# Row maxima over 97 rows with a zero row, masks in fp32r, one product for several heads, folds in turn, and another order of the streams

## What is computed

```python
scores = jnp.einsum('bqhd,bkd->bhqk', q, k) * scale        # 16 heads, one key head
scores = jnp.where(causal[None, None], scores, min_val)
attn = jax.nn.softmax(scores, axis=-1)
ctx = jnp.einsum('bhqk,bkd->bqhd', attn, v)
...
gate = x @ W_gate + _lora(x, sA_gate, sB_gate, scale) + _expert_lora(...)
up = x @ W_up + _lora(x, sA_up, sB_up, scale) + _expert_lora(...)
hidden = jax.nn.silu(gate) * up
out = hidden @ W_down + _lora(hidden, sA_down, sB_down, scale) + _expert_lora(...)
```

## Time and profile before

| | |
|---|---|
| median of 3 runs | 995.62 us (990.35 to 1001.97) |
| the profiled execution | 999.05 us |
| its span, first to last instruction | 997.3 us |
| mean granted TensorE clock | 0.962 |
| busy: PE / PEld / DVE / ACT / POOL | 938.5 / 672.2 / 614.4 / 315.5 / 310.1 us |
| fill matmuls | 428 |

### The profile page before, as it was taken

One profiled execution on the slowest core, in us unless ns is written; L12 is line 12 of the kernel. 1 busy time (PEld: TensorE's weight loads), 2 busy tenths in 40 slices (PEclk: granted clock), 3 DMA queues, 4 the chain that ended last, 5 costly groups with the idle time before them and its releaser, 6 DMA issues.

```text
span 997.3 us, 13830 instructions
## 1 busy us (share of the span) xinstructions
PE 938.5 (94%) x5362; PEld 672.2 (67%) x5370; DVE 614.4 (62%) x945; ACT 315.5 (32%) x544; POOL 310.1 (31%) x393
## 2 busy tenths in 40 slices
PE   6899998689999899999999899999989999899997
PEld 5665576445567676766687666766668787578885
DVE  2375668778876596766756785765567665332222
ACT  2323532345453116253332234334221521120110
POOL 3634631444770132235400141255114023011110
PEclk9887999698799999999999999999999999999999
DMA  8796625343790933358346533372524455535442
GB/s 288 254 313 236 246 106 131 110 129 131 277 337 18 257 107 114 139 209 300 128 156 152 177 121 123 134 276 99 204 74 185 153 192 206 190 126 193 173 162 90
DMA packets 42917, 174.96 MB, mean 175 GB/s; under 512 B 5404, under 2 KB 8220, under 8 KB 32868
## 3 DMA queue, kind: packets, MB, share of 16 engines
q1 hardware_dynamic: 36804, 119.02, 35.2%
q10 hardware_dynamic: 6048, 55.05, 15.3%
HBM read 127.46 MB, written 33.75 MB: 162 GB/s over the span
## 4 chain that ended last, share of the span: by engine, by line
PE 81%; DVE 6%; issue 3%; ACT 3%; DMA 3%; SPq 2%; POOL 1%; POOLq 0%; DVEq 0%
PE ring L984 12%; PE ring L985 12%; PE ring L986 12%; PE ring L981 5%; PE slots L1056 4%; PE av L1088 4%; PE slots L1074 4%; PE ring L1220 4%; PE den L1088 3%; PE slots L984 3%; PE slots L986 3%; PE slots L985 3%; SPq L608 2%; PE slots L1157 2%; PE slots L1053 2%
## 5 line engine op out<-in xcount | busy, mean ns | idle before, releaser
L776 POOL TENSOR_TENSOR hd_l<-hd,hd_h 128x512 fp32r<-128x512 f32 x44 | 57.3, 1302 | 287.7 <-ACT hd_h L951 287.7
L984 PE MATMUL ring<-xT_h,gu 128*128 128x512 f32 x352 | 143.2, 407 | 0.4 <-DVE gated L1544 0.3
L1338 DVE TENSOR_REDUCE negm<-slots 128x1 f32<-128x384 f32 (+3 forms) x176 | 107.2, 636 | 58.2 <-PE slots L1056 57.2
L985 PE MATMUL ring<-xT_l,gu 128*128 128x512 f32 x352 | 137.6, 391 | 0.0
L986 PE MATMUL ring<-xT_h,gu 128*128 128x512 f32 x352 | 137.5, 391 | 0.0
L853 ACT ACTIVATE probs<-slots 128x512 f32<-128x512 f32 (+1 forms) x176 | 90.7, 556 | 97.4 <-PE slots L1074 97.0
L743 POOL TENSOR_SCALAR_AFFINE_SELECT probs<-probs 128x128 f32<-128x128 f32 (+2 forms) x176 | 67.3, 394 | 125.6 <-ACT probs L853 124.8
L1056 PE MATMUL slots<-kst,qst 96*128 96x128 f32 (+3 forms) x256 | 87.2, 416 | 0.0
L1074 PE MATMUL slots<-qst,kst 98*128 98x128 f32 (+3 forms) x256 | 68.5, 357 | 13.2 <-DMA qst<-negm_hl 12.1
L984 PEld LDWEIGHTS ring<-xT_h,gu 128*128 128x128 f32 x352 | 66.3, 188 | 19.6 <-issue 7.1
L986 PEld LDWEIGHTS ring<-xT_h,gu 128*128 128x128 f32 x352 | 66.1, 188 | 14.6
(11 more groups left out here) (195 smaller groups left out, 1807.8 us busy)
## 6 DMA issues: line engine op xcount, KB each, us to landing
gu<-gu_parts ACTq DMA_DIRECT2D x42, 1280.0 KB, 5.5
dn<-dn_parts SPq DMA_DIRECT2D x12, 1728.0 KB, 7.3
gu_parts<-gu SPq DMA_DIRECT2D x11, 1280.0 KB, 5.5
qst<-qT_h SPq DMA_DIRECT2D x64, 128.0 KB, 2.4
raw_gu<-gu SPq DMA_DIRECT2D x11, 640.0 KB, 7.4
dn_parts<-dn SPq DMA_DIRECT2D x11, 576.0 KB, 7.7
dn<-dn_parts SPq DMA_DIRECT2D x4, 1152.0 KB, 5.2
x_in<-x SPq DMA_DIRECT2D x8, 512.0 KB, 5.7
```

What stands on the lines that cost most here:

```text
L776: pool.tensor_tensor(hd_l[:, i, :], hd[:, i, :], hd_h[:, i, :].bitcast(F32), ALU.subtract).then_inc(hd_lo.sem, 1)
L984: pe.matmul(out_, w_hi_, m_hi_, start=start, stop=False, skip_group_check=True)
L985: pe.matmul(out_, w_hi_, m_lo_, start=False, stop=False, skip_group_check=True)
L1338: dve.tensor_reduce(negm[:, h0:h0 + heads, qt], slot("max", b, g, i)[:, 0, 0:heads * n].rearrange("p (h n) -> p h n", n=n), AX.X, ALU.max, ...
```

## The change

Five edits. (1) A 97th row (`MROW`) goes between the 96 rows and the maxima: zero in `kst`, and in `qst` rows of the identity, which the zeros cancel. The maxima's products run over 97 rows, the scores' over 99. Two more DMAs per `q` step write that row, ahead of the 12. (2) Identity and mask of the maxima are fp32r (`mask_r`) instead of bf16; a bf16 identity (`ident_bf`) stays for fills and transposes. (3) `scores` issues one matmul for all heads of a bank: one of 4 x 128 columns instead of four (16 banks), one of 2 x 256 instead of two (32 banks). (4) `prep_gu` claims both PSUM tiles first and goes from side to side, tile by tile. (5) `TURNS` is another: 439 fills instead of 428, mostly as many short ones, and steps in another order.

```diff
+MROW = KROWS + 1
...
-    "A1A111114111111111114111111414111AA4444111111111111194111141AA1114A14AAAAA1AAA1W41WWAAWAX14XX11X1114X1XXX41XXW"
+    "A11A111411111411111111111AA111111111111111141111111111111111111114111111111111111111111111AA11A11AA11AAA111111"
...
-        mask_bf = sb("mask_bf", [P, 2, P], BF16)
+        ident_bf, mask_r = sb("ident_bf", [P, 1, P], BF16), sb("mask_r", [P, 2, P], F32R)
...
-        q_moved, m_moved = [sig(f"q_moved{i}", 16 * 12) for i in range(2)], [sig(f"m_moved{i}", 32) for i in range(4)]
+        q_moved, m_moved = [sig(f"q_moved{i}", 16 * 14) for i in range(2)], [sig(f"m_moved{i}", 32) for i in range(4)]
...
+                for g in (2 * ep, 2 * ep + 1):
+                    sp.dma_start(qst[KROWS:MROW, 4 * g:4 * g + 4, :].bitcast(F32), mask_r[0:4 * TT, 0, :].bitcast(F32)).then_inc(q_moved[ep].sem, 16)
...
-                for src, row in ((negm_h, KROWS), (negm_l, KROWS + 1)):
+                for src, row in ((negm_h, MROW), (negm_l, MROW + 1)):
...
-                                              (kst[KROWS:P, :].bitcast(F32), 1.0), (ln_eps[:, :], LN_EPS))):
+                                              (kst[KROWS:P, :].bitcast(F32), 1.0), (kst[KROWS:MROW, :].bitcast(F32), 0.0), (ln_eps[:, :], LN_EPS))):
...
-                for side in range(2):
-                    rank_rows = slice(32 * side, 32 * side + RANK)
-                    ps = in_ring.claim(pe, ("prep_gu", f, side), folded_gu, 2 * f + side + 1)
-                    for k in range(KT):
-                        mm = pe.matmul(ps[:, k * P:(k + 1) * P], fold[rank_rows, k * P:(k + 1) * P],
+                ps = [in_ring.claim(pe, ("prep_gu", f, side), folded_gu, 2 * f + side + 1) for side in range(2)]
+                for k in range(KT):
+                    for side in range(2):
+                        rank_rows = slice(32 * side, 32 * side + RANK)
+                        mm = pe.matmul(ps[side][:, k * P:(k + 1) * P], fold[rank_rows, k * P:(k + 1) * P],
...
-                pe.matmul(diagonal, mask_bf[:, 0, :], mask_bf[:, 1:2, :].to_broadcast([P, heads, P]), start=True, stop=False,
+                pe.matmul(diagonal, mask_r[:, 0, :], mask_r[:, 1:2, :].to_broadcast([P, heads, P]), start=True, stop=False,
...
-                    mm = pe.matmul(ps[:, 0, h * n:(h + 1) * n], qst[0:KROWS, 4 * g + h0 + h, qt * P:(qt + 1) * P],
-                                   kst[0:KROWS, 0:n], start=False, stop=True, skip_group_check=True)
+                    mm = pe.matmul(ps[:, 0, h * n:(h + 1) * n], qst[0:MROW, 4 * g + h0 + h, qt * P:(qt + 1) * P],
+                                   kst[0:MROW, 0:n], start=False, stop=True, skip_group_check=True)
...
-                for h in range(heads):
-                    mm = pe.matmul(ps[:, 0, h * n:(h + 1) * n], kst[0:KROWS + 2, kt * P:(kt + 1) * P],
-                                   qst[0:KROWS + 2, 4 * g + h0 + h, kt * P:T], start=True, stop=True, skip_group_check=True)
-                mm.then_inc(t_ps.sem, 1)
+                pe.matmul(ps[:, 0, 0:heads * n].rearrange("p (h n) -> p h n", n=n), kst[0:MROW + 2, kt * P:(kt + 1) * P],
+                          qst[0:MROW + 2, 4 * g + h0:4 * g + h0 + heads, kt * P:T], start=True, stop=True, skip_group_check=True)\
+                    .then_inc(t_ps.sem, 1)
```

More of the change, by code:

```diff
@@ L285 @@
[L285 to L289, removed]
@@ new lines @@
+    "WXWXAX1AXXAXWXXAAAAA11111AA111111AX11XAA1AA1AAAAA41XAAX1AAAAAAAAAAA14111A41111WAAAAAAWA1141AAAA11A4111A11A141A"
+    "11AAAA11AAAWWAAAA4A1AA44AAAAAAAA111AAAAA11AAAWAAAAAAAAAWALWALLA444AL4L4L1L1L41A4AALAA4LLA444LXXLWXLLX4LX4LXXX1"
+    "1LX1XLLXX4LLXALX444X49LAXL1ALLX4LAX1XALLWLXWLWXXALLWLLLLLLXLALWXAXXALAAAAAXALAXAXXLAAAXALLLA4AXLXAAL4ALAAALLAL"
+    "AAAAAAAXALLAAAXXALLLWAAAAXAALLWLLAWXLLWLLLLLAXWXXALAXWLALXX9ALLAALAF9AAAWAAAAALAALAWAALLWWALFFLAAAAFALAAAFAAAA"
+    "FAALALAAWAAAALFAALAAAAAFAFAFAFAAFAFLFALAA1FL111ALAFLFFFFXXXFFXXFFFLFXF1XXFXFFFFLF4XFFFALFFF1XFFFFLAFXFF1XXFFFA"
@@ new lines @@
+    "XXAFFALLFLFXFXAXLFFXXXXFFLLX1LLFAAXFAFLAXFFFFLLALFFLFFFFAFFLLFAFXXLFFLFXFLFFALLXXFALFFFFFAXFFAFFLXLFFXFFXLXLL1"
+    "XLAFXLL1ALFFLLFFFLFFLLFLFAAFFXFAALLALFFAFFLAAFLALAFFFFLALFAAALAFFFALFXFAAAAAXF1ALXFFFAFAFFAXXFLFLFALAAFLFLAAAA"
+    "AFFAAFLLLLAFFLLAFFLLFLALLFLAFFFFFLAFAFFAAFALFFFAFALFAAFAFFALLFFLFLFFALALAAFLAFAFFFLFLAAFFFAAFFLFAAAAAAAAALFFAF"
+    "AFAAFAFAAAFAAAAAFFAAFAFFFLFAFF1LFAFFFFAF1FFFAFFAFFFFAFFXFLFFFXXAFFFXXXFFFXXXFLXFLFFXFAFXFXFXFFXFAFXLFXFLFFFFFX"
+    "XFFFXFFXXAXFAFALLFFFFXFFFFFLLLFFLXAAFXFFFLLFL1LAXLFLFFXFFFXFFXFFLLFLFXAXLXFXFFAFFLLLFFFAFAXLAAAFXFLFXLLFFLLXFF"
@@ new lines @@
+    "FFAAFXLXXLFFLLLLLFLLLAFLFALAFAF1AAFLFFLFFLLFFAAAFLFFL1LAAALAALLAFFLFFFLLAFXFAFFFFFLAAAFFLFLFLFLAFFLLLFFFFLFLFF"
+    "FALFLLFAFALLLLFAFFFAFLFALFLFLFFLFAAAFLLXAXAAFFFFFFFFFALFLAAAALLAAAFFAAFFFAAAAAAFAAFFAFALFAAAAAALFAFAAAAFFAAAAF"
+    "FAFAAAAFAAFFFAAFAAFFAFAFFFFAFAFFFFFFFFFAFAAFFFFFLFAFLLFFFF9FLFFFFFLLFFLFFFFFFFFFFLFLFFFFFFFLFLLFFFFFFFLFFFFLFF"
+    "LFLFFLLFLLLFFFFLFFFLFFFLFLFFFFFLLLFLLFFFFFFFLLFFLFLFFLLLFFFLFLFLFLFFLLFFFFFFFFFLFFLFFFFLLFLLFFFFLFLLLFLFFFFLFL"
+    "FFFFFLFFLFFFLFFFFLFFLLFLLLLLLFFLFLFFLFFFLLFFLFLLFFFFFLFFFFFFFFLFFFFFFFFFFFFLFFFLFFLFFLLFLFLLFFF4FFFFFFFFFFFFFF"
@@ L787, in _ @@
             act.wait_ge(c_loaded.sem, 32)
-            act.activation(mask_bf[:, 0, :], cst[:, :], ACT.Copy).then_inc(masks_ready.sem, 1)
-            act.activation(mask_bf[:, 1, :], masks[:, :], ACT.Copy).then_inc(masks_ready.sem, 1)
+            act.activation(ident_bf[:, 0, :], cst[:, :], ACT.Copy).then_inc(masks_ready.sem, 1)
+            act.activation(mask_r[:, 0, :], cst[:, :], ACT.Copy).then_inc(masks_ready.sem, 1)
+            act.activation(mask_r[:, 1, :], masks[:, :], ACT.Copy).then_inc(masks_ready.sem, 1)
             act.wait_ge(w_loaded.sem, 16)
@@ L974, in _ @@
             pe.wait_ge(c_loaded.sem, 32)
-            pe.wait_ge(masks_ready.sem, 2)
+            pe.wait_ge(masks_ready.sem, 3)
             def fill(n):
@@ L980, in fill @@
                 for _ in range(n):
-                    pe.matmul(ps[:, 0:2 * P], mask_bf[:, 0, :], mask_bf[:, :, :], start=True, stop=True, skip_group_check=True)
+                    pe.matmul(ps[:, 0:2 * P], ident_bf[:, 0, :], ident_bf[:, :, :].to_broadcast([P, 2, P]), start=True, stop=True, skip_group_check=True)
             def three(out_, w_hi_, w_lo_, m_hi_, m_lo_, start, stop):
```

22 lines of the change are left out of this document (7 added, 15 removed).

## The result

The changed kernel takes 1002.78 us (median of 20 runs); the kernel before, measured beside it, 1003.48 us (median of 20). The ratio is 1.0059, 95% interval 1.0031 to 1.0086. Forecast were 979 us and a range of 961 to 1000, so the forecast was wrong. The change makes no difference of 1%: by the ratio it is a loss of 0.3 to 0.9%, by the medians nothing.

The account below looks back on a forecast made before the run. TensorE was taken to bound the kernel from 280 us on, a mixture with 74 us at half clock before. Terms -3 - 6 - 2 + 3.7 + 1.2 - 3 - 8 = -17.1 from 995.6 gave 979 us, range 961 to 1000.

Parts of the forecast that it names:

- the longest wait: TensorE's 8.86 us wait for batch 1's maxima shrinks to 1 to 2 us: -3 us, bounds -15 and +10.
- a new wait behind 300 us: Sign against the forecast: a wait there, where nothing covers it, would break the forecast altogether; no size given.
- rival B: Gain before 280 us is absorbed as waits for VectorE, ScalarE or DMAs: -5 us, 990.5 us, chance 0.26.
- The clock: Before 280 us, fewer waits, shorter folds and fills return part of the half-clock time: -8 us, bounds 0 and -25.
- Rival C: Clock holds 2.4 GHz nearly throughout: -25 us instead of -8, 961 us, chance 0.12.
- Folds in turn: Eleven fold steps: both sides' matmuls overlap throughout, 16 take 0.9 us instead of 1.5: -6 us, bounds 0 and -8.
- Scores: Score banks: one product for four heads pays one weight load, 16 banks x about 0.2: -3 us, bounds -4 and -2.
- Masks: 176 banks of the maxima: fp32r mask product is shorter, its wider weight load hidden under the matmul ahead: -2 us.
- rival A: Load of the fp32r identity lies open at each of 176 banks, 25 us in all: 1005 us, chance 0.10.
- The 97th row: Two more DMAs per query move delay the first maxima of batches 0 to 2: +3.7 us, bounds 0 and +5.
- Fills: 11 more at 0.11 us: +1.2 us; 36 more up to batch 0's first gate product, 25 fewer behind it.
- The base: Median of the kernel before from which the terms were subtracted: 995.62 us, of three runs.

Follow-up runs that it names:

- the new back of the order: Changed kernel with the old order up to the last output product of batch 1's attention, the new order behind it: 999.34 us, ratio 0.9985.
- the front: Changed kernel with the new order up to the last output product of batch 1's attention, the old order behind it: 1001.12 us, ratio 1.006.
- the halves: Kernel before with only the new order: 1020.67 us, ratio 1.0205; changed kernel with the old order, so only the edits: 991.05 us, ratio 0.9937.

## Why the prediction was wrong, step by step

**The step that failed is "the longest wait"**, and in it the sentence "Other waits move too, and the order can't say how far". I gave the whole new order -3 us and bounds of -15 and +10. The runs give it +20 us in the kernel before and +12 with the edits in, outside these bounds. I had followed one wait out of the order and taken it for the order's worth. Most of what the order costs in the kernel before is not even waiting in itself: 18.1 of 24 us in the ledger are half clock on work and 4 are idle time. With the edits in, the ledger shows 6 of the 12: 4 idle, 2 half clock, 3 work, less 3 of fills.

The new waits of the changed kernel are 3.92 us for `negm_hl` at 257, 2.61 for POOL's probabilities at 481, 1.95 at 117, and 1 us more for `hd_l` at 854. None of them stands in the trace of before, so a reading of that trace could not price them. The last sentence of the prediction said what would break it, a new wait behind 300 us. It did come, and the new back of the order costs some 3 to 5 us at the same clock; the larger part, 8 to 10, lies in the front. Which of the new waits costs what wasn't tested one by one.

**Even the wait that went gave nothing.** It is gone in the changed kernel:

```profile
186.34 0.27 ACT L847 ACTIVATE negm_hl<-slots 16x128 fp32r<-16x128 f32 x1 [9.01 <-PE slots L1069]
188.14 0.28 DVE L1348 TENSOR_TENSOR negm_hl<-slots,negm_hl 16x128 fp32r<-16x128 f32 x1
188.49 1.20 SPq L621 DMA_DIRECT2D qst<-negm_hl  x2
...
190.98 0.50 PE L1079 MATMUL slots<-qst,kst 99*128 99x512 f32 x1
```

5 us behind the turn instead of 9, with 25 fills in between, as worked out. The integer product of batch 0 starts at 207.3 us, as it did before: rival B's mechanism, at this place. (The turn itself came 2 us later than before, at 185.93.)

**The clock** (-8). The sign was right, and the median clock rose by 0.012, which is 11 us by the table above, more than I gave. But it is the work of the edits alone: the order by itself lowers it (0.957 to 0.9505), which the forecast has nowhere. And against the profile from which the sum was made, half clock on work fell by only 2.8 us. Rival C's clock without breaks didn't come.

**Folds in turn** (-6). The 16 matmuls take 1.16 us instead of 1.71 at full clock, 0.55 gained, as worked out. In the changed kernel three of the eleven steps lie at half clock, where they take 2.08, more than the 1.71 of before, when all but a bit of one step ran at full clock:

```profile
38.13 1.16 PE L999 MATMUL ring<-fold 8*128 8x128 f32 x16
```

```profile
171.54 2.08 PE L999 MATMUL ring<-fold 8*128 8x128 f32 x16
```

Alone, with one step at half clock, the folds shorten the eleven steps from 18.9 us to 13.7; in the changed kernel they are at 15.7. The ledger gives the folds alone 4.4 us less work and 3.2 less half clock, and 3.3 more idle time; the runs at the same clock are 1 us faster. So the step itself was sized nearly right, and what failed is that it would reach the end of the kernel: much of it came back as waits, as rival B has it.

**Scores** (-3): right, 2.8 in their own matmuls (46.9 to 44.1 at full clock), 4 at the same clock; four heads now take 0.23 us. **Masks** (-2): behind a product of 512 columns the bank of 384 columns takes 0.29 us where it took 0.30:

```profile
414.73 0.22 PE L1059 MATMUL slots<-mask_r 128*128 128x128 f32 x1
414.79 0.39 PE L1062 MATMUL slots<-kst,qst 97*128 97x384 f32 x1
415.01 0.63 PE L1225 MATMUL ring<-y_u,gu 128*128 128x512 f32 x2
```

0.28 from this bank to the next matmul where the earlier trace rows have 0.29. Right behind wide products, and invisible in the whole. The load of the identity did double,

```profile
L1059 PEld LDWEIGHTS slots<-mask_r 128*128 128x128 f32 x176 | 36.0, 204 | 35.3 <-issue 20.6 <-DVE negm L1343 5.5 <-ACT probs L858 2.2
```

204 ns where 104 were, and it lies under the products only where a long one stands ahead. The kernels with and without the mask edit, both with scores and folds in the old order, have the same matmul ahead of each bank. Here it is a short one, `av` with 128 columns, first with the bf16 mask, then in fp32r:

```profile
202.56 0.42 PE L1088 MATMUL av<-probs,v 128*32 128x128 f32 x8
202.91 0.23 PE L1054 MATMUL slots<-mask_bf 128*128 128x128 bf16 x1
202.95 0.48 PE L1057 MATMUL slots<-kst,qst 96*128 96x512 f32 x1
203.36 0.43 PE L1088 MATMUL den<-probs,ones 128*32 128x128 f32 x8
```

```profile
201.19 0.42 PE L1089 MATMUL av<-probs,v 128*32 128x128 f32 x8
201.54 0.33 PE L1055 MATMUL slots<-mask_r 128*128 128x128 f32 x1
201.71 0.45 PE L1058 MATMUL slots<-kst,qst 96*128 96x512 f32 x1
202.09 0.42 PE L1089 MATMUL den<-probs,ones 128*32 128x128 f32 x8
```

From `av` to `den` 0.80 us became 0.90. Of the 176 banks 110 ran at full clock and without a wait in both traces. From the start of the matmul ahead to the start of the one behind, the 28 behind another bank's products are 0.026 us shorter in the mean, those behind products of the feed-forward 0.009 to 0.015, the 11 behind `av`, `den` and the folds 0.09 to 0.10 longer, and the 5 behind the transposes 0.06 longer. In the mean of all 110 that is +0.001 us: the two cancel. So rival A's mechanism is real at one bank in seven, its price of 25 us is excluded, and the term was 0 instead of -2.

**The 97th row** (+3.7): the issues were sized right, 1.2 us in each batch, but in four batches and not in three: with all edits and the old order batch 3 waits 1.49 us instead of 0.32, and in the changed kernel 1.83, where I took it for covered. 4.8 us of idle time, 3.9 by medians. Two more entries stand at the head of the move:

```profile
33.44 1.21 SPq L608 DMA_DIRECT2D qst<-mask_r  x2
34.70 0.68 SPq L612 DMA_DIRECT2D qst<-qT_h  x1
```

**Fills** (+1.2): the count was right, and 10.42 us of them are left behind 280 us, 2.9 less than in the earlier trace rows, as worked out. Idle time there grew by more (28.1 to 33.9 us).

**The base.** 995.62 us was 6 us below what 81 runs give. With the right base the same terms would have given 985, still 18 us below what was measured.

## What to carry to other kernels

A changed order of a full schedule is the largest term and the least known: price it by what it could cost at every place where TensorE is the bound, not by the one wait that it removes, and leave both signs open. Before a wait is called removed, follow every engine of its chain, not only the one that the trace names; here a second one stood behind it. Before a weight load is called hidden, look at the shortest matmul that can stand ahead of it, not at the usual one. Compare runs at the same granted clock as well as medians: a gain by clock and a loss by order cancelled here within 1 us, and only the halves showed both. But don't take a higher mean clock for a gain: where fills raised it by 0.012, the time fell by 2 us.

## What the runs showed of the hardware

A wait of 2.4 to 4.1 us in an otherwise full stage can be followed by TensorE at 1.2 GHz on full work. In the changed kernel, around 325 us:

```profile
320.00:325.00 5.00, 4.84 (x22) 3.68 (x20) 3.94 (x8) 1.74 (x3) 0.00 (x0) 1.00 0.83 182
325.00:329.00 4.00, 0.07 (x1) 0.10 (x1) 0.61 (x2) 0.00 (x0) 0.00 (x0) 0.98 0.86 191
329.00:333.00 4.00, 4.00 (x15) 3.62 (x16) 2.02 (x3) 0.00 (x0) 0.00 (x0) 0.50 1.01 313
333.00:337.00 4.00, 4.00 (x15) 3.39 (x14) 2.92 (x4) 0.63 (x1) 1.30 (x1) 0.66 1.11 243
```

The clock is full in the wait and falls behind it, at 328.9 us. A wait of 2.38 us at 854 in this kernel was followed by 3.4 us at half clock, one of 2.61 us at 481 by none. The wait for the queries of batch 2 was 2.71 us in the kernel with scores and folds and was followed by nothing of the kind (nor were the 2.68 us of the kernel before); in the kernel with the folds alone it was 2.71 us as well, and 6.8 us at half clock followed. So the wait alone doesn't decide it; what else does stays open. Open too is which moves of the table cost most: the front half does more than the back, and no single step was isolated.
